# A decoder kernel: experts chosen pair by pair, picks summed by two additions, one-hots numbered by ScalarE

## The reference

```python
# block 5: y = Wd[e] (silu(x Wg[e]) * (x Wu[e])), e from the token id; then x = layernorm(x + y)
# block 6, routing:
logits = x2d @ gate_w.T                         # 1024 x 32
rw = softmax(logits)
scores = sigmoid(logits)
_, sel = top_k(scores, 4)
w = take_along_axis(rw, sel); w = w / w.sum()   # weights of the 4 picks
# then every (token, pick) pair goes through its expert (inter 96) and through
# the small expert sel // 2 (inter 128), weighted and summed
```

## Time and profile before

| | us |
|---|---|
| median of 3 runs (858.33 to 860.5) | 858.41 |
| the profiled execution, whole | 859.32 |
| its span in the trace | 857.4 |
| PE busy in the span | 767.4 |
| DVE busy | 612.8 |
| ACT busy | 455.8 |
| POOL busy | 432.6 |

### The profile page before, as it was taken

One profiled execution on the slowest core, in us unless ns is written; L12 is line 12 of the kernel. 1 busy time (PEld: TensorE's weight loads), 2 busy tenths in 40 slices (PEclk: granted clock), 3 DMA queues, 4 the chain that ended last, 5 costly groups with the idle time before them and its releaser, 6 DMA issues. The chain is left out here.

```text
span 857.4 us, 18273 instructions
## 1 busy us (share of the span) xinstructions
PE 767.4 (90%) x5842; PEld 483.8 (56%) x5842; DVE 612.8 (71%) x2052; ACT 455.8 (53%) x1447; POOL 432.6 (50%) x428
## 2 busy tenths in 40 slices
PE   6999989897959999999999999999894699999943
PEld 3766666665834444555555555787674555555523
DVE  1666777796856777898888888342345778888956
ACT  2387787673431001888888888100333087777724
POOL 4355565562004666766666666000630478888840
PEclk9999999999979999999999999999996599999977
DMA  9400000000004666300000000240378222222225
GB/s 323 189 2 2 2 2 1 2 1 1 1 14 101 166 171 152 99 2 2 1 1 1 2 1 1 109 206 18 107 260 211 104 63 76 75 79 72 73 64 190
DMA packets 32237, 63.17 MB, mean 74 GB/s; under 512 B 6592, under 2 KB 21068, under 8 KB 31280
## 3 DMA queue, kind: packets, MB, share of 16 engines
q1 hardware_dynamic: 20704, 41.40, 15.1%
q0 software_dynamic: 4896, 11.95, 4.5%
q10 hardware_dynamic: 6544, 8.67, 3.8%
HBM read 41.01 MB, written 9.84 MB: 59 GB/s over the span
## 5 line engine op out<-in xcount | busy, mean ns | idle before, releaser
L1418 ACT ACTIVATE a_room<-a_room,a_nm 128x257 f32<-128x257 f32 x256 | 127.3, 499 | 100.6 <-DVE a_nm L1261 99.8
L1460 POOL TENSOR_TENSOR a_room<-a_room,a_rd 128x1024 f32<-128x1024 f32 x64 | 121.3, 1895 | 65.8 <-DVE a_rd L1269 65.4
L1261 DVE CUSTOM_DVE_ANT_0 a_room<-a_ps,table,NSK 128x256 f32<-128x256 f32 x256 | 107.8, 478 | 0.4 <-PE a_ps L1120 0.4
L836 ACT ACTIVATE l_Pr<-l_Sm,l_nm 128x128 f32<-128x128 f32 (+1 forms) x192 | 88.3, 461 | 32.9 <-DVE l_nm L656 18.9
L922 POOL TENSOR_TENSOR l_Pr<-l_Pr,l_rd 128x256 f32<-128x256 f32 (+1 forms) x80 | 82.0, 1043 | 46.7 <-DVE l_rd L670 46.5
L1120 PEld LDWEIGHTS a_ps<-room 64*128 64x128 f32 x512 | 44.1, 186 | 53.2 <-issue 48.5
L1120 PE MATMUL a_ps<-room 64*128 64x256 f32 x512 | 72.3, 402 | 0.5 <-DVE a_nm L1261 0.5
L1200 PE MATMUL a_ps<-a_room,W 128*128 128x512 f32 x160 | 71.2, 602 | 0.8 <-ACT a_room L1432 0.8
L1241 DVE SCALAR_TENSOR_TENSOR a_room<-a_ps,BQK,table 128x512 f32<-128x512 f32 x80 | 56.4, 746 | 20.6 <-PE a_ps L1200 20.6
L1135 PE MATMUL a_ps<-table,a_room 128*128 128x128 f32 x512 | 69.7, 279 | 1.1 <-ACT a_room L1427 1.1
L1148 PE MATMUL a_psO<-a_room,room 128*64 128x512 f32 x256 | 68.8, 617 | 0.0
(11 more groups left out here) (323 smaller groups left out, 1780.6 us busy)
## 6 DMA issues: line engine op xcount, KB each, us to landing
room<-a_room SPq DMA_DIRECT2D x96, 64.0 KB, 2.0
room<-a_room ACTq DMA_DIRECT2D x96, 64.0 KB, 2.1
room<-in_w_in SPq DMA_DIRECT2D x1, 6144.0 KB, 18.3
room<-in_c_in SPq DMA_DIRECT2D x1, 4096.0 KB, 15.3
room<-pairs SPq DMA_DIRECT2D x8, 512.0 KB, 8.0
W<-in_w SPq DMA_DIRECT2D x1, 3072.0 KB, 12.4
room<-in_w_out SPq DMA_DIRECT2D x1, 3072.0 KB, 20.0
W<-in_wo SPq DMA_DIRECT2D x1, 2048.0 KB, 8.4
```

What stands on the lines that cost most here:

```text
L836: nc.scalar.activation(Pr[:, t % 4, n, 0:n_keys], Sm[:, t % 2, n, 0:n_keys], ACT.Exp, bias=nm[:, t % 2, n:n + 1], scale=-1.0, accum_out=de ...
L1261: nc.vector.tensor_tensor_reduce(out=Sm[:, t % 2, n, 0:S], in0=psS(t)[:, n // 2, n % 2, :], in1=c["window"][:, n % 2, :], scale=-1.0, scal ...
L1418: nc.scalar.activation(Pr[:, t % 4, n, :], Sm[:, t % 2, n, :], ACT.Exp, bias=nm[:, t % 2, n:n + 1], scale=-1.0, accum_out=den[:, t % 2, n: ...
L1460: pool.tensor_tensor(p, p, rd[:, t % 2, :].unsqueeze(2).to_broadcast([P, 4, S]), ALU.mult).then_inc(normed, 1)
```

## The change

Four edits. The logits of pairs 0 to 3 go to te_psL, the two halves of te_psH and te_psY, and ACT forms exp and copy of each pair as soon as it is there (`keep_logits`). DVE does the sigmoid, the largest 8 and their positions pair by pair at the end of `token_experts`, not in `route`. The sum over the four picks becomes two additions, the second with bf16 output. The numbering of ro_in_tile moves from POOL (4 operations of 8 x 40) to ACT (32 scalings of 40, each by a number a partition).

```diff
@@ -1513,7 +1513,10 @@
         back = [st.sem("te_back%d" % g) for g in range(G)]
         scattered = st.sem("te_scattered")
         s = {n: st.sem("te_" + n) for n in ("xT", "xt", "h", "sg", "a", "aT", "at", "down", "taken", "stat", "mixed",
-                                           "std", "rstd", "normed", "zT", "zt", "logits")}
+                                           "std", "rstd", "normed", "zT", "zt", "logits", "exp", "rank")}
+
+        def logits_of(g):
+            return (psL[:, 0:2 * NE], psH[:, 0, 0:2 * NE], psH[:, 1, 0:2 * NE], psY[:, 0, 0:2 * NE])[g]
         block = stack.enter_context(nc.Block())
 
         @block.sync
@@ -1598,9 +1601,13 @@
                 pe.wait_ge(s["zt"], g + 1)
                 if g == 0:
                     pe.wait_ge(loads["gate"], 16)
+                if g == 1:
+                    pe.wait_ge(s["a"], NSORT)
+                if g == 3:
+                    pe.wait_ge(s["taken"], NSORT)
                 for t in range(2):
                     for kk in range(KD):
-                        last = nc.tensor.matmul(psL[:, (2 * g + t) * NE:(2 * g + t + 1) * NE], zT[:, g % 2, t, kk, :],
+                        last = nc.tensor.matmul(logits_of(g)[:, t * NE:(t + 1) * NE], zT[:, g % 2, t, kk, :],
                                                 GW[:, kk, :], start=(kk == 0), stop=(kk == KD - 1))
                 last.then_inc(s["logits"], 1)
 
@@ -1637,6 +1644,13 @@
                 need(act, s["logits"], g - 1)
                 nc.scalar.activation(zT[:, g % 2], psX[:, g % 2, :].rearrange("p (t k q) -> p t k q", t=2, k=KD),
                                      ACT.Copy).then_inc(s["zt"], 1)
+
+            def keep_logits(g):
+                act.wait_ge(s["logits"], g + 1)
+                pair = slice(2 * g, 2 * g + 2)
+                raw = logits_of(g).rearrange("p (t e) -> p t e", t=2)
+                nc.scalar.activation(tiles.sc[:, pair, :], raw, ACT.Exp, scale=-1.0).then_inc(s["exp"], 1)
+                nc.scalar.activation(tiles.lg[:, pair, :], raw, ACT.Copy)
 
             nc.scalar.activation(warm[:, 0:1], c["ones"][:, 0:1], ACT.Sqrt)
             act.wait_ge(scattered, 16 * NSORT)
@@ -1652,12 +1666,11 @@
             nc.scalar.activation(warm[:, 1:2], c["ones"][:, 0:1], ACT.Exp)
             keep_z(1)
             keep_z(2)
+            keep_logits(0)
             keep_z(3)
-            act.wait_ge(s["logits"], G)
-            nc.scalar.activation(tiles.sc[:, :, :], psL[:, 0:NT * NE].rearrange("p (t e) -> p t e", t=NT),
-                                 ACT.Exp, scale=-1.0)
-            nc.scalar.activation(tiles.lg[:, :, :], psL[:, 0:NT * NE].rearrange("p (t e) -> p t e", t=NT),
-                                 ACT.Copy)
+            keep_logits(1)
+            keep_logits(2)
+            keep_logits(3)
 
         @block.vector
         def _(dve):
@@ -1686,6 +1699,18 @@
                 for t in range(2 * g, 2 * g + 2):
                     nc.vector.tensor_scalar(X[:, t, :], R[:, t, 0:D], R[:, t, D:D + 1], rstd[:, t:t + 1],
                                             ALU.subtract, ALU.mult).then_inc(s["normed"], 1)
+            link = Chain(dve, s["rank"]).link
+            sc = tiles.sc
+            for g in range(G):
+                pair = slice(2 * g, 2 * g + 2)
+                dve.wait_ge(s["exp"], g + 1)
+                link(nc.vector.tensor_scalar(sc[:, pair, :], sc[:, pair, :], 1.0, None, ALU.add))
+                link(nc.vector.reciprocal(sc[:, pair, :], sc[:, pair, :]))
+                for t in range(2 * g, 2 * g + 2):
+                    last = nc.vector.max(tiles.top[:, t, :], sc[:, t, :])
+                link(last)
+                for t in range(2 * g, 2 * g + 2):
+                    nc.vector.max_index(tiles.idx[:, t, :], tiles.top[:, t, :], sc[:, t, :])
 
 
 
@@ -1702,9 +1727,7 @@
         st = Store(nc, stack)
         PAIRS = TOPK * NT
         nmx = st.sb("ro_nmx", [P, NT])
-        picks = st.sb("ro_picks", [P, NT, NE])
-        top = st.sb("ro_top", [P, NT, 8])
-        idx = st.sb("ro_idx", [P, NT, 8], U32)
+        picks = st.sb("ro_picks", [P, 2, NT, NE])
         idf = st.sb("ro_idf", [P, NT, 8])
         lg, sc, ex, sel = tiles.lg, tiles.sc, tiles.ex, tiles.sel
         picked = st.sb("ro_picked", [P, TOPK, NT, NE])
@@ -1772,36 +1795,25 @@
             act.wait_ge(s["shift"], 1)
             for t in range(NT):
                 nc.scalar.activation(ex[:, t, :], lg[:, t, :], ACT.Exp, bias=nmx[:, t:t + 1])
-
-        @block.gpsimd
-        def _(pool):
             for k in range(TOPK):
-                which = slice(k * NT, (k + 1) * NT)
-                pool.wait_ge(s["located"], k + 1)
-                pool.tensor_tensor(in_tile[:, which, :], in_tile[:, which, :].bitcast(F32),
-                                   c["pairs"][:, which].unsqueeze(2).to_broadcast([P, NT, NTILE]),
-                                   ALU.mult).then_inc(s["numbered"], 1)
+                act.wait_ge(s["located"], k + 1)
+                for i in range(k * NT, (k + 1) * NT):
+                    last = nc.scalar.activation(in_tile[:, i, :], in_tile[:, i, :].bitcast(F32), ACT.Copy,
+                                                scale=c["pairs"][:, i:i + 1])
+                last.then_inc(s["numbered"], 1)
 
         @block.vector
         def _(dve):
             link = Chain(dve, s["dve"]).link
             link(nc.vector.memset(ends[:, :, :], 0.0))
 
-            link(nc.vector.tensor_scalar(sc[:, :, :], sc[:, :, :], 1.0, None, ALU.add))
-            link(nc.vector.reciprocal(sc[:, :, :], sc[:, :, :]))
-            for t in range(NT):
-                last = nc.vector.max(top[:, t, :], sc[:, t, :])
-            link(last)
-            for t in range(NT):
-                last = nc.vector.max_index(idx[:, t, :], top[:, t, :], sc[:, t, :])
-            link(last)
-            link(nc.vector.tensor_copy(idf[:, :, :], idx[:, :, :]))
+            link(nc.vector.tensor_copy(idf[:, :, :], tiles.idx[:, :, :]))
             link(nc.vector.tensor_tensor(
                 sel[:, :, :, :], c["slots"][:, 0:NE].unsqueeze(1).unsqueeze(1).to_broadcast([P, TOPK, NT, NE]),
                 idf[:, :, 0:TOPK].rearrange("p t k -> p k t").unsqueeze(3).to_broadcast([P, TOPK, NT, NE]),
                 ALU.is_equal))
-            link(nc.vector.tensor_reduce(picks[:, :, :], sel.rearrange("p k t e -> p t e k"), AX.X, ALU.add))
-            nc.vector.tensor_copy(chosen[:, :, :], picks[:, :, :]).then_inc(s["chosen"], 1)
+            link(nc.vector.tensor_tensor(picks[:, :, :, :], sel[:, 0:2], sel[:, 2:4], ALU.add))
+            nc.vector.tensor_tensor(chosen[:, :, :], picks[:, 0], picks[:, 1], ALU.add).then_inc(s["chosen"], 1)
 
             nc.vector.tensor_reduce(nmx[:, :], lg[:, :, :], AX.X, ALU.max, negate=True).then_inc(s["shift"], 1)
             dve.wait_ge(s["ranked"], 1)
@@ -1904,6 +1916,8 @@
         self.index = st.sb("ti_index", [P, NTILE, 2], U32)
         self.weight = st.sb("ti_weight", [P, TOPK, NT])
         self.total = st.sb("ti_total", [P, NT])
+        self.top = st.sb("ti_top", [P, NT, 8])
+        self.idx = st.sb("ti_idx", [P, NT, 8], U32)
 
     def take(self, spare):
         n = NT * NE
```

## The result

The changed kernel takes 855.26 us (median of 10 runs, 852.52 to 857.31); the kernel before, beside it, 859.66 (10 runs, 858.33 to 862.15). That is 4.4 us less. The profiled execution took 855.28, its span 853.4.

What follows compares the result with a forecast made beforehand. A single file of waits among PE, ACT and DVE from the last logits to experts was taken as the bound. 3.16 + 1.08 + 0.62 = 4.86 us off 859.32 gave 854.46, 853.6 for the median; range 852.0 to 856.2.

Steps and rivals of the forecast that it cites:

- The file of work: From PE's last logits to experts, engines wait in single file, so each us taken out should come off whole.
- Part A: Choice moved from route to pair-by-pair groups ahead of the barrier; cast of the positions starts 3.16 us earlier.
- The group that was forecast at 1.46: DVE's work for one pair: addition, reciprocal, two MAX8 and two positions, together 1.46 us.
- the interpolated reciprocal: DVE's reciprocal over 64 elements, taken between rows of 256 and 8: 0.55 us, plus a link of 0.04.
- The queueing of group 3 behind group 2: DVE's last pair's group starts at 653.19, when the third's ends, its exp being ready at 652.96.
- Part B: Sum over the picks in route, as two additions of 1.13 us instead of 2.21: saves 1.08 us.
- Part C: Numbering of the one-hots in the pick loop by ACT instead of POOL: PE ends 0.62 us earlier.
- turn-taking: In the pick loop DVE and POOL alternate at shared ports; without POOL, DVE's step is 1.54 us.
- No release: Pick loop: one-hots of picks 1 to 3 keep 1.0 us; gain 4.1, time 854.3; chance 0.06.
- Not hidden: DVE's four groups start only after the last logits; gain 0.7 us, time 857.7; chance 0.05.
- Slower: Pick loop: ACT's 32 scalings do not overlap, 0.494 us each; net 3.7 slower, 862.1 us; chance 0.05.
- Clock: Pick loop: closer packing restores PE's higher clock, last pick costs about half; time 852.5 us; chance 0.05.

Runs made afterwards that it cites:

- e1: Kernel before with only the choice pair by pair, its sum and numbering kept; 856.76 us against 860.23, ratio 0.9964.
- e4: Changed kernel with the numbering given back to POOL; ratio to the kernel before 0.9955.
- e5: Changed kernel, but DVE starts its four groups of choice only when all four pairs' exponentials are there; ratio to the kernel before 0.9998.
- e2: Kernel before with only the sum over the picks made by two additions; ratio 0.9987.
- e6: Changed kernel plus one POOL multiplication into an unread scratch tile beside each pick's numbering; one execution, products end 0.95 us later.
- e11: Changed kernel with e9's filler matmuls plus 7, 4, 12 and 3 at four places from the last logit through route; ratio to the kernel before 0.9925.
- e3: Kernel before with only the numbering moved, ACT's 32 scalings replacing POOL's four operations; ratio 0.9994.
- e7: Changed kernel with each scaling also done once into a scratch tile, 64 in all; one execution, 860.27 us.
- e10: Changed kernel with filler matmuls only from the last logit on and through route (2, 3, 10 and 2); ratio to the kernel before 0.9935.
- e12: e11 with 6, 5, 12 and 4 fillers through route and one between the picks of the loop; 854.11 us against 860.08, ratio 0.9918.
- e9: e8 with fewer filler matmuls, 19, 1 and 1 where that has 21, 4 and 2; ratio to the kernel before 0.9924.
- e8: Changed kernel with 11 more filler matmuls between the turns and logits of the token experts' tail; ratio to the kernel before 0.9959.

## Why the prediction was right, point by point

**The file of work.** Right: what was taken out between the last logit and ti_index came off nearly in full (4.94 in the profile, 4.4 in the medians). e1 to e4 show the parts adding up.

**Part A**, 3.16 forecast, 3.10 measured, and 3.10 again in e1. The group that was forecast at 1.46 takes 1.46 to 1.48, with the interpolated reciprocal at 0.55. The queueing of group 3 behind group 2 happened as worked out. That it is cover and not less work, e5 shows.

**Part B**, 1.08 forecast, 1.07 measured; 1.06 in e2. The output in bf16 costs what it does in f32 (0.42).

**Part C**, 0.62 forecast, 0.77 measured. Two steps were right (first pick 0.18 later; one-hots back to 0.49, by turn-taking, e6). One was off: I added 0.02 of waiting to PE's eight loads and named PE, at 1.80, as what binds the step. The step is 1.75, and three steps of 0.05 less are the 0.15 by which C came out larger; e11 shows that ACT sets the step, for it stays when PE's matmuls of a pick take 1.07 instead of 1.90.

**The rivals.** No release: refuted by e3, where the one-hots take 0.48 without POOL, and by e6, where they take 1.0 again with it. Not hidden: e5 makes it happen and measures it, A -1.12 where I had -1.0. Slower: refuted, a scaling is 0.218; e7 doubles them and loses 7.0. Clock: it did not rise in the loop of the changed kernel. The price I gave it, a last pick at half cost, is not tested: in e10 the clock fell behind the first pick, in e11 behind the second, in e12 just before the last, which cost 1.90 in all three. That the higher level alone does not speed up the other picks is shown.

**What was not foreseen.** I held the end of the logits fixed. In the profiled execution it came 0.68 later after the same start: 0.51 of it because PE's clock fell earlier in the tail, 0.17 because te_R's last part came later. e9 shows that with the clock held this stretch is 8.4 instead of 11 to 11.7. That the last tile of experts regained 0.83 of the 1.77 lost up to the last logit is luck.

My forecast of 853.6 stood on a median of three runs, 858.41; over ten it is 859.66. Of the 1.7 us between forecast and result 1.25 are this, and 0.46 is the gain, which was 4.4 where I had 4.86. The result, 855.26, lies above the 852.4 to 855.0 that I had worked out for the forecast case and inside the range only because that was widened to 856.2 for the rivals. The terms of the gain were nearly right; that the time fell into the range is in part the width that I gave to cases which did not occur. Why PE's clock falls earlier in one execution than in another, and what moves the first te_std by 1 to 3 us between executions, no run here settles.

## What to carry to other kernels

Work that one engine does behind another's last result is worth most if it can start with the first part of that result: here the smaller pieces cost 1.1 us more and still won 3.1, and moving one wait gave all of it back. The operation on POOL beside DVE cost DVE 0.5 us of its own row, and POOL's long row (1.63 us) is mostly waiting, as read from the ends in e6. Many small scalings on ACT were better here because their step, 0.219 us, is under the estimated 0.24 at which the gain is gone. Where runs scatter by 4 to 5 us, as here, read edits of one microsecond from stretches between two events in the profile, and sum them before trusting a median of three.

## What the runs showed of the hardware

The loop over the picks neither brought PE's higher clock nor held it. In the changed kernel's loop PE is busy for 7.14 us without a gap and the granted clock stays 0.50, and in e12 it fell from 1.00 to 0.50 at 674 though PE had been busy 4.67 of the 5.00 us before. What would have held it is open.

An ACT scaling over 40 elements, one number a partition, has a row of 0.31 to 0.33 us, but back to back the starts follow at 0.218 to 0.219. In e7, where scalings from f32 to f32 and from f32 to fp32r alternate, both have the same.

A filler of 256 columns in fp32 stands in the trace as two matmuls: the four of e8 are a row of x8, 1.89 us.
